# Routing weights turned into rows by VectorE's block transpose and eight transfers, in place of TensorE and ScalarE

## What is computed

```python
def _route(xf, router_w, correction_bias):
    logits = xf @ router_w.T
    scores = jax.nn.sigmoid(logits)
    ...
    _, topk_idx = jax.lax.top_k(masked, K)          # 4 of 16 experts, from 2 of 4 groups
    w = jnp.take_along_axis(scores, topk_idx, axis=1)
    w = w / (w.sum(axis=-1, keepdims=True) + 1e-20)
combine = jnp.zeros((S, E), xf.dtype).at[jnp.arange(S)[:, None], topk_idx].add(w)
g = jnp.einsum('sc,ech->esh', xf, gate_w)
u = jnp.einsum('sc,ech->esh', xf, up_w)
h = jax.nn.silu(g) * u
hw = h * combine.T[:, :, None]
routed = jnp.einsum('esh,ehc->sc', hw, down_w)
return (shared_out + routed).reshape(B, T, C)
```

## Time and profile before

| | |
|---|---|
| three runs, us | 932.68, 938.91, 941.02; median 938.91 |
| profiled execution, us | 936.66 |
| its span, us | 934.8, 19500 instructions |
| granted TensorE clock, mean | 0.991 of full speed |
| TensorE busy | 882.2 us (94%) |
| VectorE busy | 620.9 us (66%) |
| ScalarE busy | 434.5 us (46%) |
| GpSimd busy | 230.1 us (25%) |
| DMA packets | 36105, 39.21 MB |

### The profile page before, as it was taken

The page is one execution under the profiler, slowest core; times in us unless marked ns, Lnnn a source line. Parts: engine busy times, 40 slices in busy tenths (PEclk is TensorE's granted clock), DMA queues, the critical chain, the costliest instruction groups (busy, mean ns, idle before and its releaser), DMA issues.

```text
span 934.8 us, 19500 instructions
## 1 busy us (share of the span) xinstructions
PE 882.2 (94%) x7856; PEld 783.3 (84%) x7856; DVE 620.9 (66%) x1629; ACT 434.5 (46%) x843; POOL 230.1 (25%) x198
## 2 busy tenths in 40 slices
PE   5788879999999999999999999999999999999997
PEld 3576657998988888898988889888888989988997
DVE  6638886777785479755786467754787647764532
ACT  2534633851574336642465425643366434722442
POOL 2114201232311243113321224122331133122232
PEclk9999799999999999999999999999999999999999
DMA  6000320120002100210002010020101200120121
GB/s 234 1 1 1 129 66 1 47 72 24 24 27 70 34 26 12 72 36 24 23 13 84 23 35 24 26 72 20 39 13 49 59 1 23 31 77 25 33 71 34
DMA packets 36105, 39.21 MB, mean 42 GB/s; under 512 B 3248, under 2 KB 32432, under 8 KB 36016
## 3 DMA queue, kind: packets, MB, share of 16 engines
q1 hardware_dynamic: 36016, 37.96, 13.0%
HBM read 32.97 MB, written 4.98 MB: 41 GB/s over the span
## 4 chain that ended last, share of the span: by engine, by line
PE 82%; DVE 8%; ACT 4%; issue 3%; DMA 2%; POOL 1%; SPq 0%; POOLq 0%; DVEq 0%
PE ring L1361 8%; PE g_ps L517 5%; PE d_ps L517 5%; PE g_ps L519 4%; PE g_ps L518 4%; PE u_ps L517 4%; PE u_ps L519 4%; PE u_ps L518 4%; PE d_ps L519 4%; PE d_ps L518 4%; PE ring L1229 4%; PE num L1258 3%; PE ring L1454 3%; PE ring L1344 3%; PE ring L519 3%
## 5 line engine op out<-in xcount | busy, mean ns | idle before, releaser
L701 POOL TENSOR_TENSOR hl<-hb,hh 128x512 fp32r<-128x512 f32 x96 | 126.5, 1318 | 404.7 <-ACT hh L839 404.7
L839 ACT ACTIVATE hh<-hb 128x512 fp32r<-128x512 f32 x96 | 60.6, 632 | 177.3 <-DVE hb L1201 165.0
L517 PE MATMUL d_ps<-hh,down_h 128*128 128x256 f32 x384 | 114.7, 299 | 3.3 <-POOL hl L701 3.2
L1196 DVE TENSOR_TENSOR hb<-sl,u_ps 128x512 f32<-128x512 f32 x88 | 60.1, 683 | 79.5 <-PE u_ps L519 36.3
L517 PE MATMUL g_ps<-normed_h,gate_h 128*128 128x256 f32 x352 | 106.6, 303 | 3.4 <-DVE hb L1196 3.4
L518 PE MATMUL d_ps<-hl,down_h 128*128 128x256 f32 x384 | 107.7, 280 | 0.0
L519 PE MATMUL d_ps<-hh,down_l 128*128 128x256 f32 x384 | 107.5, 280 | 0.0
L519 PE MATMUL g_ps<-normed_h,gate_l 128*128 128x256 f32 x352 | 99.8, 283 | 0.0
L518 PE MATMUL g_ps<-normed_l,gate_h 128*128 128x256 f32 x352 | 99.3, 282 | 0.0
L519 PE MATMUL u_ps<-normed_h,up_l 128*128 128x256 f32 x352 | 99.2, 282 | 0.0
L518 PE MATMUL u_ps<-normed_l,up_h 128*128 128x256 f32 x352 | 99.0, 281 | 0.0
(11 more groups left out here) (403 smaller groups left out, 2112.7 us busy)
## 6 DMA issues: line engine op xcount, KB each, us to landing
weights_over_hidden<-weights_by_expert SPq DMA_DIRECT2D x128, 128.0 KB, 3.0
shared<-denominators_by_head SPq DMA_DIRECT2D x16, 256.0 KB
out_x<-kept SPq DMA_DIRECT2D x16, 256.0 KB, 2.2
x_s<-in_x SPq DMA_DIRECT2D x12, 256.0 KB, 3.1
raw_weights<-in_gateT SPq DMA_DIRECT2D x4, 384.0 KB, 6.6
raw_weights<-in_upT SPq DMA_DIRECT2D x4, 384.0 KB, 5.7
raw_weights<-in_down SPq DMA_DIRECT2D x4, 384.0 KB, 8.3
cheb_s<-in_cheb SPq DMA_DIRECT2D x3, 256.0 KB, 5.3
```

The lines of the kernel that those rows point to most:

```text
L517: eng.matmul(ps, wh, xh, start=start, stop=False, **how)
L701: pool.tensor_tensor(hl[:, j % 2, :], hb, hh[:, j % 2, :].bitcast(F32), ALU.subtract).then_inc(*ffn_pool.mark(p, f"lo{j}"))
L839: act.activation(hh[:, j % 2, :], hb, ACT.Copy).then_inc(*ffn_act.mark(p, f"hi{j}"))
L1196: dve.tensor_tensor(hb, sl, gate_up(p, j)[1][:, :], ALU.mult).then_inc(*ffn_dve.mark(p, f"h{j}"))
```

## The change

The step `cb` leaves TensorE and ScalarE. VectorE turns `wsel`, 128x64, by one instruction that transposes each block of 32x32 on its own. In the result, partition 32a + 16q' + e holds expert e, and its columns are two pieces of 32 tokens. Eight transfers of 16 partitions each, two pieces of 32 numbers (128 bytes) in each partition, put the pieces in place in `rows_kept`, and SP waits for all eight. The tensor in memory is the same as before, and so is all behind it.

VectorE's transpose waits for the stores of the pair before and for its own L1187. In the lists `cb` now stands right behind `r4`: in the body before `prod`, where it stood behind it, in the opening and the closing ahead of the attention steps `k0` to `q0` of the next pair or of two feed-forward steps. The wait of `V00` is now for the logits to have been read.

```diff
-    +1 tok0 lg +1 gn tok1 +3 nrm xg +2 r1 xl0 +1 xT0 xl1 M +2 xT1 r2 k0 k1 v1 q0 v0 r3 +2 Y0 silu +1 r4 prod cb Epre
-    Eexp kt q1 +2 Erep dent kv +1 rd lr +2 S00 +1 V00 +1 p2 +4 S01 +2 sp0 rv0 sp1 +1 st0 +2 at0 rv1 +1 V01 +1 S10 +1
+    +1 tok0 lg +1 gn tok1 +3 nrm xg +2 r1 xl0 +1 xT0 xl1 M +2 xT1 r2 k0 k1 v1 q0 v0 r3 +2 Y0 silu +1 r4 cb prod Epre Eexp
+    kt q1 +2 Erep dent kv +1 rd lr +2 S00 +1 V00 +1 p2 +4 S01 +2 sp0 rv0 sp1 +1 st0 +2 at0 rv1 +1 V01 +1 S10 +1 Y1 +1 V10
...
             def keep_rows(p):
-                sp.wait_ge(route_act.of(p), route_act.at(p, "cb"))
-                sp.dma_start(rows_kept[p % 2], comb[:, :]).then_inc(rows_written, 16)
-                sp.wait_ge(rows_written, 16 * (p + 1))
+                sp.wait_ge(route_dve.of(p), route_dve.at(p, "cb"))
+                by_block = rows_kept[p % 2].rearrange("e (h q a t) -> a q e h t", h=2, q=2, a=4)
+                for a in range(4):
+                    for q in range(2):
+                        first = 32 * a + EXPERTS * q
+                        sp.dma_start(by_block[a, q], turned[first:first + EXPERTS, :].rearrange("e (h t) -> e h t", h=2)).then_inc(rows_written, 16)
+                sp.wait_ge(rows_written, ROWS_OF_PAIR * (p + 1))
...
-                if name == "cb":
-                    if p:
-                        act.wait_ge(rows_written, 16 * p)
-                    act.activation(comb[:, :], t[0:EXPERTS, :], ACT.Copy).then_inc(*route_act.mark(p, "cb"))
...
+                if name == "cb":
+                    if p:
+                        dve.wait_ge(rows_written, ROWS_OF_PAIR * p)
+                    own(rt, p, "wn")
+                    dve.transpose(turned[:, :], wsel.rearrange("p q e -> p (q e)")).then_inc(*rt.mark(p, "cb"))
...
-                    pe.wait_ge(route_act.of(p - 1), route_act.at(p - 1, "cb"))
+                    pe.wait_ge(route_dve.of(p - 1), route_dve.at(p - 1, "logits"))
...
-                if name == "cb":
-                    pe.wait_ge(route_dve.of(p), route_dve.at(p, "wn"))
-                    for q in range(4):
-                        last = pe.transpose(t[0:EXPERTS, q * P:(q + 1) * P], wsel[:, q, :], ident)
                     last.then_inc(*route_pe.mark(p, name))
```

More of the change, by code:

```diff
@@ L29 @@
 BIG = 3e30
+ROWS_OF_PAIR = 8 * 16
 UNCHOSEN = -1e30
@@ L118 @@
 OPENING = """
[L119 to L128, removed]
@@ L129 @@
-    1:kt +3 1:q1 +2 2:tc1 +1 0:low13 1:dent +2 1:kv +1 1:rd +2 1:S00 +4 0:exp 1:V00 +2 2:z1 1:S01 +2 1:at0 +2 1:V01 +1
-    1:S10 +3 1:V10 +1 1:S11 +1 1:V11 +1 2:z2 1:at1 +2 2:z3 +1 1:wo0 1:wo1 +3 1:tk0 1:tk1 +4 1:nrm2 +2 1:xn0 1:xn1
-    1:exp +1
+    0:gn 0:xg 0:hot0 0:xT0 1:gn 1:xg 0:M 0:xT1 1:xT0 0:high0 0:hot1 0:hot2 0:Y0 2:gn 1:M 1:xT1 0:hot3 0:prod 0:Epre 0:hot4
+    0:Eexp 0:high1 0:hot5 1:Y0 1:prod 2:xg 1:Epre 0:Erep 0:lr 0:hot6 1:Eexp 0:high2 2:xT0 0:p2 1:Erep 2:M 1:lr 0:sp0
+    0:low0 0:hot7 0:rv0 0:xb 1:p2 0:sp1 0:st0 0:hot8 0:rv1 0:hot9 0:Y1 0:hot10 0:st1 0:o0 2:xT1 1:sp0 0:o1 0:tc0 1:rv0
@@ new lines @@
+    1:sp1 1:st0 0:tc1 0:high3 2:Y0 0:hot11 0:z1 0:hot12 1:rv1 2:prod 0:z2 0:low1 1:Y1 0:hot13 1:st1 0:z3 1:o0 2:Epre 1:o1
+    2:Eexp 0:tok0 0:tok1 1:tc0 1:tc1 0:nrm 1:xb 1:z1 2:Erep 0:xl0 0:xl1 1:z2 2:lr 0:hot14 0:k0 1:z3 0:k1 0:v1 0:q0 0:v0
+    0:kt 0:q1 0:high4 2:p2 0:hot15 0:hot16 0:high5 0:dent 0:kv 0:rd 0:low2 0:high6 0:S00 0:hot17 0:high7 2:sp0 0:V00 0:S01
+    0:hot18 0:high8 0:hot19 0:low3 0:low4 0:at0 0:high9 2:rv0 0:hot20 0:V01 0:S10 0:hot21 2:sp1 2:st0 0:V10 0:low5 0:S11
+    2:rv1 0:low6 0:hot22 0:V11 0:high10 0:at1 2:Y1 0:high11 0:wo0 0:wo1 0:hot23 0:tk0 0:tk1 0:nrm2 2:st1 2:o0 0:xn0 0:xn1
@@ L132 @@
+    0:low7 1:tok0 1:tok1 0:low8 0:lg 0:r1 1:nrm 0:r2 0:low9 0:low10 +2 2:o1 +1 2:xb 0:r3 1:xl0 1:xl1 2:tc0 +1 0:low11
+    0:high12 0:silu 0:low12 0:high13 0:r4 0:cb 1:k0 +1 1:k1 1:v1 1:q0 +1 1:v0 1:kt +3 1:q1 +2 2:tc1 +1 0:low13 1:dent +2
+    1:kv +1 1:rd +2 1:S00 +4 0:exp 1:V00 +2 2:z1 1:S01 +2 1:at0 +2 1:V01 +1 1:S10 +3 1:V10 +1 1:S11 +1 1:V11 +1 2:z2 1:at1
+    +2 2:z3 +1 1:wo0 1:wo1 +3 1:tk0 1:tk1 +4 1:nrm2 +2 1:xn0 1:xn1 1:exp +1
 """
 BODY = """
-    +1 tok0 lg +1 gn tok1 +3 nrm xg +2 r1 xl0 +1 xT0 xl1 M +2 xT1 r2 k0 k1 v1 q0 v0 r3 +2 Y0 silu +1 r4 prod cb Epre
@@ L138 @@
 """
 CLOSING = """
[L141 to L144, removed]
+    +1 7:tok0 7:tok1 +2 7:nrm +3 6:lg +1 6:r1 +1 7:xl0 7:xl1 6:r2 +1 6:r3 6:silu +1 6:r4 6:cb +2 7:k0 7:k1 7:v1 7:q0 7:v0
@@ L145 @@
+    7:kt 7:q1 +3 7:dent 7:kv +2 7:rd +1 7:S00 +2 7:V00 7:S01 7:at0 +1 7:V01 +1 7:S10 +4 7:V10 7:S11 +1 7:V11 +1 7:at1 +1
+    7:wo0 +2 7:wo1 7:tk0 7:tk1 +4 7:nrm2 +2 7:xn0 +6 7:xn1 +4 7:lg 7:r1 +4 7:r2 +2 7:r3 7:silu +2 7:r4 7:cb +3 +16 7:exp
+    +29
 """
@@ L360, in graph_attention_moe @@
         wsum = sb("wsum", [P, 4])
-        comb = sb("comb", [EXPERTS, 512])
+        turned = sb("turned_weights", [P, 4 * EXPERTS])
         dens_kept = nc.dram_tensor("denominators_by_head", (2, 32, 512), F32).ap()
@@ L819, in route @@
             def route(p, name):
-                t = num
-                if name == "cb":
-                    act.wait_ge(route_pe.of(p), route_pe.at(p, name))
                 if name == "lg":
```

10 lines of the change are left out of this document (4 added, 6 removed).

## The result

The changed kernel takes 966.15 us, the median of four executions (964.04, 965.81, 966.49, and a slow one of 1122.6 at a granted clock of 0.745, without which the median is 965.81), the kernel before beside it 938.97: a ratio of 1.029 from the other three, with an interval of 1.023 to 1.036. That is **27.2 us slower**. The forecast was 7.8 slower (946.7), its range ended at 956: the sign was right, the size was not.

A forecast was written before the change was run, and what follows sets the result against it. The prediction took TensorE's own sequence as the bound, with rows 1.5 us later in pairs 1 to 5: 2.2 + 4.5 + 1.8 - 0.7 = 7.8 us slower, added to the median for 946.7 us, range 941 to 956.

The forecast's parts named there:

- What bounds the kernel, where it is late: TensorE, busy 94% of the span; it stalls when broadcast weight rows come late, and a late product is paid in full.
- What is removed: PE transposes and ScalarE copy: worth 0 in pairs 1 to 5, 0.35 us each in pairs 0 and 6.
- The VectorE transpose: One added 128x64 instruction on VectorE, 0.23 us, fitting into idle time before te and costing 0 there.
- The landing: Time for the last of eight small writes to reach memory: 1.7 us, upper bound 2.9.
- The pitch of the eight writes: Time between two issues on SP's queue: 0.42 us, bounds 0.38 and 0.62.
- each transfer is dear: Rival: each write's issue takes L620's 0.62 us, delay 2.9 us, sum 16.7 us, 956 us; chance 0.12.
- The price of a microsecond: What late rows cost TensorE: 1.5 us of delay in pairs 1 to 5, 1.8 in pair 7, sum 7.8 us slower.
- TensorE has 0.43 us of slack and pays the rest: Rule from pair 4: L1201 shifted by 1.77 us, the down projection by 1.34, the turn 1.5 us longer.
- Pair 7: Rows 1.8 us later, all paid because TensorE already stalls 2.2 us at the down projection; saved transposes return as waiting.
- faster: Rival: issues on SP of 0.2 us or less bring rows earlier and shrink stalls; 3.5 us gained, 935.4; chance 0.05.
- hidden anyway: Rival: delay up to 0.4 us nearly meets the slack, pairs 1 and 2 lose nothing; 938 to 940 us; chance 0.13.
- The base: Forecast added to the median 938.91 us, 2.25 above the profiled execution; the 8 us spread ascribed to late landings.

The follow-up runs named there:

- after: The changed kernel, with VectorE's transpose and eight writes of the rows, against the kernel without the change: 966.15 us against 938.97, ratio 1.029.
- one_store: The changed kernel with one write of all 128 partitions in place of eight, order mended at L1201: 935.84 us against 938.15; a repeat 933.98 against 937.53.
- before: The kernel without the change, with PE transposes, ScalarE copy and one write of the rows: 938.97 us beside the changed kernel.
- eight_padded: The changed kernel with rows in memory 640 numbers apart instead of 512, so that nothing folds: 950.19 us against 937.53, ratio 1.013.
- apart_5: delay_5 with a third, unused piece in each row of the unread destination, so that rows and pieces don't fold: 965.98 us against 937.59, one execution.
- long_5: apart_5 with pieces of 128 numbers (512 bytes) in place of 32: 958.98 us against 937.59, one execution.
- eight_flat: The changed kernel with each row of its eight writes one contiguous 256-byte piece, token order left wrong: 952.97 us against 938.79, one execution.
- delay_2: The kernel without the change, plus two unread writes of the new form ahead of its one write: 946.85 us against 938.15, ratio 1.009.
- experiment 3: The kernel without the change, delayed by two, three or five unread writes ahead of its one write: 946.85, 955.58 and 969.87 us.
- four_stores: The changed kernel with four writes of 32 partitions in place of eight of 16: 935.44 us against 938.15, ratio 0.997.
- plain_5: delay_5 with its five unread writes as plain contiguous copies of whole 2 KB rows: 963.22 us against 938.79, ratio 1.025.
- delay_5: The kernel without the change, plus five unread writes of the new form ahead of its one write: 969.87 us against 938.15, ratio 1.032.
- delay_3: The kernel without the change, plus three unread writes of the new form ahead of its one write: 955.58 us against 938.79, ratio 1.017.

## Why the prediction was right or wrong

- **What bounds the kernel, where it is late: right.** The way from the weights to the broadcast rows decides, and a late product is paid in full. The growth lies in the two stalls that were named and in what follows them, but for 2.7 us of longer waits at Epre, which the transposes gone from TensorE's work outweigh.
- **What is removed: right in the five pairs.** In after the wait at Epre is 4.4 us in five instead of 1.7, 0.88 in pair 1, as forecast: the transposes' time is waited out there. te was not pushed: L931 still has 0.28 us idle before it. In pair 0 the forecast gain of 0.35 did not come (96.3 us from its instruction to pair 1's in both kernels); in pair 6, one_store is 0.5 faster than before.
- **The VectorE transpose: right**, 0.24 us against 0.23.
- **The landing: right**, 1.8 against 1.7, with pieces of 128 bytes; in eight_padded, with the same pieces in another spacing, it is 1.4. The rule of the Trainium skill ("DMA: Bandwidth & Descriptors", section Specifications) that a transfer under 512 B is handled as a read-modify-write shows no price here: apart_5's 128-byte pieces land in 1.4 us, long_5's 512-byte ones in 1.5, and the whole rows in 1.6.
- **The pitch of the eight writes: wrong, and this is the step that failed.** The text took 0.42 from L600 and L591, "small and plain like L600". It measured 0.63 (5.03 us for eight). The write was not plain: a row in two pieces, in a spacing that folds with the rows. The row that it came out like was L620 with its 0.62, which has two pieces to a partition too (line 619), and which stood as a bound and as the rival *each transfer is dear*, at a chance of 0.12. Whether L620 is long for the same reason no run shows. In its pitch and delay that rival is what happened: its delay of 2.9 came out as 3.2. The estimate of 0.42 was true of the other form (eight_flat, eight_padded), and worth 14.5 us.
- **The price of a microsecond: right up to the delay that was forecast, wrong above.** For 1.5 us of delay it was 7.8 against 8.7 measured (delay_2). At 3.2 the same rule gives 2 x 2.8 + 3 x 3.2 + 3.4 - 0.7 = 17.9 where 27.2 were measured. Its stalls, 18.6 without the 0.7, came out right in sum, for the two grew by 18.0 us (22.9 less 4.9), though partly by errors that cancel: pairs 3 to 5 got 6.7 us more and not 9.6, since the late landings of pairs 4 and 5 in before were already paid, and pair 6, put at 0, got 1.8. What is missing is the clock: some 7 us by the table of experiment 3, 11.0 by the profiles. In the profiles the account closes: 18.0 of stalls, 11.0 of slower products and 2.7 more of waiting at Epre, less 3.5 for the transposes that are gone, make the 28.2 by which turns 1 to 7 are longer. The step at fault is the rule taken from pair 4, "TensorE has 0.43 us of slack and pays the rest": that turn was 1.5 us longer, its clock stood at 1.00, and I drew the line on past it. The dear rival left the clock out too: its delay was nearly right, its 16.7 us ten too few.
- **Pair 7: the size right, the reason wrong.** The 2.2 us stall, by which all of pair 7's delay was to be paid, is the one before the end, some 40 us behind the rows, and it is 2.16 in before and in after. Where pair 7's rows are first used, before doesn't stall at d_ps; after stalls 4.0 us for 3.4 of delay. That the delay is paid in full was right by luck.
- **The rivals on the fast side.** The *faster* rival had its place right (below 1.4 us for the writes): one_store's way is 2.7 us and its time 0.3 and 0.55% lower. Its price was about right too, 3.5 us against 2.3 and 3.6 in the two measurements, though 2.2 of the 4.9 us of stalls that it counted on are the stall before the end, which stays in one_store too. The forecast of "hidden anyway" is what four_stores shows nearly: a way of 4.5 us is not hidden (TensorE waits 6.0 us at d_ps, 3.8 without the stall before the end), but it costs no more than before's late landings did.
- **The base.** The 2.25 us between the profiled execution and the median were put down to late landings. They go with the clock: 0.991 in the profiled one, 0.987 in the mean of 25, which by the line is 2.5 us.
- **Chances.** The forecast had 0.60 and the dear case 0.12. Of the rows that it was priced from, L620 (0.62) has two pieces to a partition like the new write, and L600 (0.34) one. That was a reason to give the dear case more, though no row settled it.

## What to carry to other kernels

Before pricing a transfer by the nearest row, compare its form on both sides (partitions, pieces, spacing in memory), not the tile and the queue alone: after's 0.59 and eight_padded's 0.42 us differ by nothing but the spacing of rows in memory, and eight in a row multiply it. A step that is split into many transfers on one queue lies in full on the path of whoever waits for the last; one transfer of the whole tile, with the order mended at the reader, was worth more than the removal of the unit in front. And where a delay on a feeding path reaches TensorE, the stall has a second price: look at the granted clock just behind the stall, and don't extend a linear rule past the longest stall that the trace shows at full clock.

## What the runs showed of the hardware that was not expected

- **Issue length depends on how the memory side folds.** SP's issue of a 16-partition write is 0.42 us in a train with one piece to a row (eight_flat), with two pieces that don't fold (apart_5, eight_padded), and with whole rows (plain_5); 0.59 with two pieces that fold into the rows' spacing (after, delay_5). That the unlike grouping of the two sides makes the longer issue is argued from these forms, not shown by itself.
- **The length of an issue is carried on.** A plain write is 0.34 us alone, 0.42 as the last of a train of its own kind, and 0.58 behind folded ones (L603 in delay_5, 0.580 in each pair).
- **Issue time outweighs landing.** 5.03 us of issue stand beside 1.8 of landing. The Trainium skill ("DMA: Bandwidth & Descriptors", section Issuing engines are not separate DMA queues) calls the time to initiate a DMA "usually small relative to the DMA itself"; for small transfers this trace disagrees: one write's 0.59 us is a third of its 1.8, and in a train of eight the issues are the larger part.
- **Half clock behind a stall.** After 2.9 us of stall with one short group of products between, the clock is 1.2 GHz instead of 2.4 for over three microseconds, and the products of the turns of pairs 1 to 3 are busy 1.2 to 1.6 us longer than in one_store for it. Between 1.7 and 2.4 us of stall it fell in some turns and stayed at 2.4 GHz in others, with stalls alike to 0.1 us (eight_padded, pairs 3 and 4). The runs don't settle what decides.
- **The spread of a kernel's executions is the clock.** 933 to 945 us for the same instructions go with a mean clock of 0.996 to 0.977 in a line. In the profiles the low stretches of before and of the kernels with little stall lie in the opening (0.87 to 0.96 in 80 to 120 us), outside the change. I had put the spread down to late landings of rows, which was wrong. What makes the opening's clock differ is open.
- **Slow single issues, left open.** In all trains of eight or five, and in delay_2 and delay_3 with three and four writes, two or three single issues last 1.2 to 1.9 us, which makes the rows of that pair up to a microsecond late (pairs 3, 4 and 6 of after, 3 and 4 of eight_padded). Wherever that happens, the write just ahead of such an issue lands late too, at 2.6 to 3.2 us. before, one_store and four_stores show none. No run tells its cause. The ways of 5.0 to 5.5 in pairs 4 and 5 of before are late landings; their cause is open too.
